# A graph-and-experts kernel: eight column sums of the count matrix move from GpSimd to VectorE, between its comparisons

## The chip, the cores and the metric

The kernel runs on one core of a Trainium2 chip. The metric is the device time of one execution in microseconds (us), the median of three runs. The profile is of one execution, taken by the hardware profiler. The engines are called TensorE (PE in the rows, PEld for its weight loads), VectorE (DVE), ScalarE (ACT), GpSimd (POOL) and SyncE (SP, which here only issues DMAs).

## The reference

The input x has 1250 nodes of 512 features; src and dst name 40,000 edges, sorted by dst. Two residual layers follow each other:

```python
def gnn(x):                                  # on layernorm(x)
    h = relu(x @ W1 + b1) @ W2 + b2          # 512 -> 256 -> 512
    agg = segment_sum(h[dst], src, 1250)     # edge_index = (src, dst)
    return h + agg
x = x + gnn(layernorm(x))

def moe(t):                                  # on layernorm(x), 8 experts of 512 x 512
    gate = softmax(t @ W_gate + b_gate)
    adapted = gate - 0.25 * sigmoid(t @ W_thr + b_thr)
    weights = max(adapted, 0) / sum          # 1 where the sum is 0
    return sum_e weights[e] * (t @ W_exp[e] + b_exp[e])
x = x + moe(layernorm(x))
```

With A[d, s] the number of edges from src s to dst d plus the identity, the aggregation is a product with A, and the bias b2 enters each node once for each edge and once for itself: it is multiplied by the column sums of A. These column sums are what the change is about.

## The kernel before

The 1250 nodes are 10 tiles of 125. Row tile i of A is built from five windows of 25 destination rows, so there are 50 windows, `w` from 0 to 49, and tile i consists of windows 5i to 5i+4.

For each window the engines do this:
- VectorE, `compare(w)` (line 556): equality comparisons (line 570) of the edge keys with the positions of the window. They write one-hot blocks in f16 into the ring `hot`. A window has 3 parts up to window 8, then 2 parts: 4 and 4 blocks up to window 17 (125x1536 elements each), 3 and 3 up to window 29 (125x1152), 3 and 2 from window 30 on (125x1152 and 125x768). From window 9 on, the ring has four places, so that `compare(w)` waits until TensorE has used the blocks of window w-4 (`freed_by`, line 569). It also waits for `pos_ready`, the positions that ScalarE prepares five windows ahead.
- TensorE, `count(w)` (line 780 on): an opening matmul (line 791), one matmul for each block (line 798), which waits for the comparison, and a closing one (line 803).
- ScalarE copies the counts from PSUM into `counts` (line 399) and then prepares positions for window w+5 (line 374).
- SyncE moves the 25 rows of the window by DMA into `a_t[i % 3]` (line 285), with one semaphore `win_moved[q]` for each of the five windows of a tile. Before the first window of a tile from tile 3 on, it waits until the buffer's last tile has been used, by `g_done` and by `a_summed` (line 284).

Between windows TensorE also does the first layer (transposes at line 755, `hidden` at line 764) and the aggregation, `aggregate` (line 776), that multiplies the relu'd features by the rows of `a_t`. Aggregation of tile i runs in five pieces behind windows 5i+8 to 5i+12, three windows behind the last window of the tile. Its fifth piece is the longest, with four matmuls.

GpSimd forms the sum of the rows of all tiles, `a_sum`, in the loop of lines 357 to 361: for tiles 1 to 8 it waits until the five windows of the tile are moved (`moved`), and adds `a_t[i % 3]` to `a_sum`, 125x1250 elements in f32. GpSimd has no other work at that time. The addition of tile 9 is on VectorE already (line 599), behind its last comparison, one low-weights step for the gate (line 589) and one for expert 0 (line 593). TensorE then reduces `a_sum` over partitions (line 819), VectorE copies the result to `deg1` (line 601) and adds b2 times it to x (line 607).

After that come the second product (line 832), the second layer norm with its transposes (line 842), the gate, and the eight experts with three matmuls for each product (lines 868 to 870).

VectorE's order of work is written out in the loop at line 581: `compare(w)`, then for some windows `statistics` or `normalise1`. Each engine executes its instructions in this order. `normalise1((w-1)//2)` follows `compare(w)` for odd w up to 19.

Of the kernel before, what the change touches and what calls it, by code (L numbers as in the profile page):

```python
# [16 lines left out]
ALU = mybir.AluOpType  # L17
# [13 lines left out]
def gnn_moe(nc, x, src, dst, W1, b1, W2, b2, Wg, bg, Wt, bt, We, be, out):  # L31
# [4 lines left out]
    TILES = 10  # L36
# [11 lines left out]
    WPT = 5  # L48
# [19 lines left out]
    with ExitStack() as ctx:  # L68
# [3 lines left out]
        def sem(name):  # L72
            return ctx.enter_context(nc.semaphore(name))
# [82 lines left out]
        a_t = [late[:, i * SW:(i + 1) * SW] for i in range(3)]  # L156
        a_sum = late[:, 3 * SW:4 * SW]
# [57 lines left out]
        a_summed = sem("a_summed")  # L215
# [20 lines left out]
        def parts_of(w):  # L236

            return next(parts for end, parts in STEPS if w < end)

        def hot_at(w, p):  # L240

            if w < EARLY:
                return 4 * (w % 2) + p
            return 2 * ((w - EARLY + 2) % 4) + p

        def freed_by(w):

            return w - 2 if w < EARLY + 2 else w - 3 if w < EARLY + 4 else w - 4

        def moved(eng, tile):  # L250

            for q in range(WPT):
                eng.wait_ge(win_moved[q], 16 * (tile + 1))
# [60 lines left out]
        @block.gpsimd  # L314
        def _(pool):
            nc.gpsimd.memset(ident[:, :], 0.0).then_inc(const_base, 1)
            nc.gpsimd.memset(ones[:, :], 1.0).then_inc(const_ready, 1)
            nc.gpsimd.memset(eps[:, :], LN_EPS).then_inc(const_ready, 1)
            nc.gpsimd.iota(base_row[:, :], pattern=[[WIN, NW]], base=0, channel_multiplier=0,
                           allow_small_or_imprecise_dtypes=True).then_inc(const_ready, 1)  # L320
            nc.gpsimd.iota(last_row[:, :], pattern=[[WIN, NW]], base=WIN - 1, channel_multiplier=0,
                           allow_small_or_imprecise_dtypes=True).then_inc(const_ready, 1)
            nc.gpsimd.iota(c_up[:, :], pattern=[[ROWS, GJ]], base=1, channel_multiplier=1,
                           allow_small_or_imprecise_dtypes=True).then_inc(const_ready, 1)
            nc.gpsimd.iota(c_down[:, :], pattern=[[-ROWS, GJ]], base=CH, channel_multiplier=-1,
                           allow_small_or_imprecise_dtypes=True).then_inc(const_ready, 1)
            pool.wait_ge(const_base, 1)
            nc.gpsimd.affine_select(out=ident[:, :], in_=ident[:, :], compare_op=ALU.not_equal, fill=1.0,
                                    base=0, pattern=[[-1, 128]], channel_multiplier=1).then_inc(const_ready, 1)

            nc.gpsimd.memset(step_col[:, :], float(sum(STEPS[-1][1]))).then_inc(step_base, 1)
            for n in range(len(STEPS) - 1, 0, -1):
                pool.wait_ge(step_base, len(STEPS) - n)
                nc.gpsimd.affine_select(out=step_col[:, :], in_=step_col[:, :], compare_op=ALU.is_ge,
                                        fill=float(sum(STEPS[n - 1][1])), base=-STEPS[n - 1][0], pattern=[[0, 1]],
                                        channel_multiplier=1).then_inc(step_base, 1)

            nc.gpsimd.iota(iota_lo[:, :], pattern=[[1, 2 * SEG]], base=0, channel_multiplier=0,
                           allow_small_or_imprecise_dtypes=True).then_inc(lo_ready, 1)
            nc.gpsimd.iota(iota_pos[:, :, 0:WIN * HI], pattern=[[0, PART], [1, WIN * HI]], base=0, channel_multiplier=0,  # L340
                           allow_small_or_imprecise_dtypes=True).then_inc(lo_ready, 1)
            nc.gpsimd.memset(iota_pos[:, :, WIN * HI:SEG], -20000).then_inc(lo_ready, 1)
            nc.gpsimd.iota(win_base[:, :], pattern=[[WIN * HI, NW]], base=0, channel_multiplier=0,
                           allow_small_or_imprecise_dtypes=True).then_inc(lo_ready, 1)
            nc.gpsimd.memset(keys[:, CH * REC:(CH + PADS) * REC], -1).then_inc(lo_ready, 1)

            nc.gpsimd.memset(zeros[:, :], 0.0).then_inc(self_ready, 1)
            nc.gpsimd.memset(self_pos[:, :], 0.0).then_inc(self_base, 1)
            nc.gpsimd.memset(self_lo[:, :], 0.0).then_inc(self_base, 1)
            pool.wait_ge(self_base, 2)  # L350

            nc.gpsimd.affine_select(out=self_pos[0:WIN, :], in_=self_pos[0:WIN, :], compare_op=ALU.not_equal, fill=1.0,
                                    base=-(HI - 1), pattern=[[1, SEG + HI - 1]], channel_multiplier=-HI).then_inc(self_ready, 1)
            nc.gpsimd.affine_select(out=self_lo[0:WIN, :], in_=self_lo[0:WIN, :], compare_op=ALU.not_equal, fill=1.0,
                                    base=-(LO - WIN), pattern=[[1, 2 * LO - WIN]], channel_multiplier=-1).then_inc(self_ready, 1)

            for i in range(1, TILES - 1):
                moved(pool, i)
                if i > 1:
                    pool.wait_ge(a_summed, i - 1)  # L360
                nc.gpsimd.tensor_tensor(a_sum, a_t[0] if i == 1 else a_sum, a_t[i % 3], ALU.add).then_inc(a_summed, 1)  # L361

        @block.scalar
        def _(act):
            act.dma_start(x_sb[112:R, :, :], x.rearrange("(t p) d -> p t d", p=R)[112:R, :, :]).then_inc(x_rest, 16)
# [101 lines left out]
        def _(dve):  # L467
# [56 lines left out]
            def statistics(half):  # L524
                for i in range(half * TILES // 2, (half + 1) * TILES // 2):
                    dve.wait_ge(x_in[i // 2], 16)
                    if i == 0:
                        dve.wait_ge(x_rest, 16)
                    nc.vector.bn_stats(stats1[:, i, :], x_sb[:, i, :]).then_inc(ln1_stats, 1)  # L529
                for i in range(half * TILES // 2, (half + 1) * TILES // 2):  # L530
                    dve.wait_ge(ln1_stats, i + 1)
                    nc.vector.bn_aggr(mv1[:, i, :], stats1[:, i, :]).then_inc(ln1_mv, 1)
# [23 lines left out]
            def compare(w):  # L556

                word = dve.snap(word_reg)
                parts = parts_of(w)
                dve.reg_add(need_reg, end_reg[freed_by(w) % 4], 1)  # L560
                dve.wait_ge(pos_ready, w + 1)
                if w < WPT:
                    dve.wait_ge(lo_ready, 6 + w)
                with dve.Fori(word % WORD, word // WORD, sum(parts) * REC) as k:
                    for p, n in enumerate(parts):
                        key_at = nc.s_assert_within(
                            k + sum(parts[:p]) * REC, 0, (CH + PADS - n) * REC,
                            skip_runtime_bounds_check_because="the table gives a block only steps that begin below CH")
                        dve.wait_ge(hot_used[p], dve.snap(need_reg))
                        nc.vector.tensor_tensor(hot[hot_at(w, p)][:, 0:n, :].rearrange("p c (k x j) -> p (c k) x j", k=SEGS, j=2),  # L570
                                                places[w % WPT][:, 0:n, :].rearrange("p c (k x j) -> p (c k) x j", k=SEGS, j=2),
                                                keys[:, ds(key_at, n * REC)].rearrange("p (k j) -> p k j", j=2).unsqueeze(2)
                                                .broadcast_to([EP, n * SEGS, SEG // 2, 2]),
                                                ALU.is_equal).then_inc(hot_ready[p], 1)

                    dve.reg_load(word_reg, wtab[0:1, w + 1:w + 2])
                    dve.reg_add(turn_reg, turn_reg, 1)
                    dve.reg_add(need_reg, turn_reg, 1)
                dve.reg_mov(end_reg[w % 4], turn_reg)

            for w in range(NW):
                compare(w)
                if w < 2:
                    statistics(w)
                if 1 <= w < 1 + 2 * TILES and (w - 1) % 2 == 0:
                    normalise1((w - 1) // 2)
# [7 lines left out]
                                               op0=ALU.mult, op1=ALU.subtract).then_inc(we_lo_done, 1)  # L594

            low_weights(0, 0)
            moved(dve, TILES - 1)
            dve.wait_ge(a_summed, TILES - 2)
            nc.vector.tensor_tensor(a_sum, a_sum, a_t[(TILES - 1) % 3], ALU.add).then_inc(a_summed, 1)
            dve.wait_ge(deg_done, 1)  # L600
            nc.vector.tensor_copy(deg1[:, :], ps_a[0:R, 0:TILES]).then_inc(deg_ready, 1)
            dve.wait_ge(deg_ready, 1)
# [326 lines left out]
```

## Time and profile before

| what | value |
|---|---|
| median of 3 runs | 419.51 us (419.5 to 421.23) |
| the profiled execution's own time | 421.23 us |
| its span in the profile | 419.4 us |
| TensorE busy | 390.8 us, 93% |
| VectorE busy | 294.9 us, 70% |
| ScalarE busy | 102.2 us, 24% |
| GpSimd busy | 26.3 us, 6% |

The span is the time from the first to the last instruction that the profile shows. Busy time is that of the instructions of an engine; register, branch, semaphore and DMA-issuing instructions are not in it. In the slices of the page, each digit is the busy share of a fortieth of the span (10.5 us) in tenths.

### The profile page before, as it was taken

To read this page: it belongs to the slowest core of one execution; us is meant where nothing else is said; L and a number is where in the kernel's file an instruction comes from. 1 tells how busy PE (TensorE), PEld (TensorE's weight loads), DVE (VectorE), ACT (ScalarE), POOL (GpSimd) and SP (SyncE) were. 2 spreads that over 40 slices of the span, in tenths; PEclk is the share of its full clock that TensorE was granted. 3 is DMA by queue.
4 is the path that set the end of the run, shared out by engine and by line. 5 is a ranking of instruction groups with operands and counts; after the bars stand their busy time and mean duration, and the time that the engine had idled before them with its cause. 6 is when DMAs were issued, how large, how long until landed. Compare 5 with 4: busy or idle time off the path is not lost.

```text
span 419.4 us, 6001 instructions
## 1 busy us (share of the span) xinstructions
PE 390.8 (93%) x1943; PEld 244.8 (58%) x1943; DVE 294.9 (70%) x438; ACT 102.2 (24%) x176; POOL 26.3 (6%) x35
## 2 busy tenths in 40 slices
PE   0845999999999999899799999999999999999996
PEld 0422676666656555546566666666666666666663
DVE  3799999945677993698359666575765757657653
ACT  4621243434456551245430101001010010100000
POOL 4000000210222223000000000000000000000000
PEclk9998699999999999999699999999999999999999
DMA  8500013214124222162001102030020300000133
GB/s 182 143 12 13 18 37 103 56 37 133 40 65 155 76 72 74 22 171 106 0 2 45 56 1 100 2 100 0 0 100 0 100 0 0 0 0 0 50 98 98
DMA packets 16681, 23.75 MB, mean 57 GB/s; under 512 B 2792, under 2 KB 9555, under 8 KB 16532
## 3 DMA queue, kind: packets, MB, share of 16 engines
q1 hardware_dynamic: 16254, 22.93, 18.7%
q10 hardware_dynamic: 403, 0.53, 0.6%
q8 instruction: 12, 0.20, 0.2%
q14 instruction: 12, 0.10, 0.1%
HBM read 14.65 MB, written 2.56 MB: 41 GB/s over the span
## 4 chain that ended last, share of the span: by engine, by line
PE 86%; DVE 8%; DMA 2%; issue 1%; DVEq 1%; ACT 1%; ACTq 0%
PE ps_g L868 17%; PE ps_g L870 17%; PE ps_g L869 17%; PE ps_w L798 10%; PE ps_g L776 10%; PE ps_a L764 5%; PE ps_g L832 2%; DVE split L570 2%; DVE x_sb L607 1%; PE ps_a L765 1%; PE ps_a L755 1%; DVE stats L529 1%; DMA dst_i<-in_dst_dram 1%; PE ps_w L791 1%; PE ps_w L803 1%
## 5 line engine op out<-in xcount | busy, mean ns | idle before, releaser
L868 PE MATMUL ps_g<-we_hi,split 128*125 128x512 f16 x320 | 122.4, 383 | 0.0
L869 PE MATMUL ps_g<-we_lo,split 128*125 128x512 f16 x320 | 122.0, 381 | 0.0
L870 PE MATMUL ps_g<-we_hi,split 128*125 128x512 f16 x320 | 122.0, 381 | 0.0
L570 DVE TENSOR_TENSOR split<-places,keys 125x1536 f16<-125x1536 int16 (+2 forms) x125 | 106.8, 916 | 17.6 <-PE ps_w L798 11.5
L681 DVE SCALAR_TENSOR_TENSOR x_sb<-ps_g,weight_s,x_sb 125x512 f32<-125x512 f32 x80 | 60.0, 750 | 56.2 <-PE ps_g L870 56.1
L798 PE MATMUL ps_w<-split 125*128 125x250 f16 x416 | 60.3, 288 | 10.8 <-DVE split L570 10.8
L686 DVE SCALAR_TENSOR_TENSOR x_sb<-late,weight,x_sb 125x512 f32<-125x512 f32 x80 | 60.0, 751 | 9.5 <-DVE x_sb L681 4.9
L798 PEld LDWEIGHTS ps_w<-split 125*128 125x128 f16 x416 | 40.5, 102 | 32.4 <-DVE split L570 19.0
L868 PEld LDWEIGHTS ps_g<-we_hi,split 128*125 128x125 f16 x320 | 44.1, 138 | 25.9 <-issue 0.6
L870 PEld LDWEIGHTS ps_g<-we_hi,split 128*125 128x125 f16 x320 | 44.0, 137 | 25.9 <-issue 0.8
L869 PEld LDWEIGHTS ps_g<-we_lo,split 128*125 128x125 f16 x320 | 44.1, 138 | 25.4 <-issue 0.6
L776 PE MATMUL ps_g<-late,r_sb 125*128 125x512 f32 (+3 forms) x120 | 53.0, 545 | 0.6 <-DMA late<-counts 0.6
L443 ACT ACTIVATE we_hi<-stage 128x2048 f16<-128x2048 f32 x6 | 11.5, 1912 | 139.4 <-PE ps_g L870 139.4
L399 ACT ACTIVATE counts<-ps_w 128x250 f32<-128x250 f32 x50 | 19.0, 379 | 70.6 <-PE ps_w L803 70.6
L374 ACT ACTIVATE places<-iota_pos,win_base 125x512 int16<-125x512 int16 x50 | 35.6, 713 | 0.0
L361 POOL TENSOR_TENSOR late<-late 125x1250 f32<-125x1250 f32 x8 | 21.2, 2649 | 135.4 <-DMA late<-counts 135.4
L776 PEld LDWEIGHTS ps_g<-late,r_sb 125*128 125x128 f32 x120 | 19.2, 189 | 10.0 <-issue 9.4
L764 PE MATMUL ps_a<-w_sb,xn_t 128*125 128x256 f32 x80 | 19.9, 392 | 0.0
L593 DVE SCALAR_TENSOR_TENSOR we_lo<-stage,we_hi 128x2048 f16<-128x2048 f32 x8 | 18.3, 2284 | 0.0
L764 PEld LDWEIGHTS ps_a<-w_sb,xn_t 128*125 128x125 f32 x80 | 14.2, 187 | 1.8
L832 PE MATMUL ps_g<-w_sb,early 128*125 128x512 f32 x32 | 14.8, 595 | 0.1
L791 PE MATMUL ps_w<-self_lo,self_pos 128*128 128x250 f16 x50 | 13.9, 278 | 0.0
(127 smaller groups left out, 200.2 us busy)
## 6 DMA issues: line engine op xcount, KB each, us to landing
stage<-in_L_ffn_W_exp_dram SPq DMA_DIRECT2D x8, 1024.0 KB, 5.3
late<-counts SPq DMA_DIRECT2D x50, 122.1 KB
x_sb<-in_x_dram SPq DMA_DIRECT2D x5, 448.0 KB, 9.4
out_dram<-x_sb SPq DMA_DIRECT2D x10, 224.0 KB
late<-in_L_ffn_b_exp_dram SPq DMA_DIRECT2D x1, 2000.0 KB
w_sb<-in_L_gnn_W_dram SPq DMA_DIRECT2D x2, 512.0 KB, 8.3
x_sb<-in_x_dram ACTq DMA_DIRECT2D x1, 260.0 KB
out_dram<-x_sb ACTq DMA_DIRECT2D x10, 26.0 KB
```

Source lines behind the costliest of these rows:

```text
L361: nc.gpsimd.tensor_tensor(a_sum, a_t[0] if i == 1 else a_sum, a_t[i % 3], ALU.add).then_inc(a_summed, 1)
L374: nc.scalar.activation(places[w % WPT][:, :, 0:SEG], iota_pos[:, :, :], ACT.Identity, bias=win_base[:, w:w + 1], scale=1.0).then_inc(pos_r ...
L570: nc.vector.tensor_tensor(hot[hot_at(w, p)][:, 0:n, :].rearrange("p c (k x j) -> p (c k) x j", k=SEGS, j=2), places[w % WPT][:, 0:n, :].re ...
L681: nc.vector.scalar_tensor_tensor(out=x_sb[:, i, :], in0=ps_exp[(TILES * par + i) % RING], scalar=weight_s[:, ds(e, 1), i], in1=x_sb[:, i, ...
L686: nc.vector.scalar_tensor_tensor(out=x_sb[:, i, :], in0=be_sb[:, ds(e, 1), :], scalar=weight[:, i, ds(e, 1)], in1=x_sb[:, i, :], op0=ALU.m ...
L764: nc.tensor.matmul(ps_a[0:R, 0:C], xn_t[:, k, :], w1_sb[:, k, :], start=(k == 0), stop=False)
L776: g = nc.tensor.matmul(ps_g[:, a:z], r_sb[:, i, c * 128:(c + 1) * 128], a_t[i % 3][:, a - c * SW:z - c * SW], start=False, stop=False, ski ...
L798: mm = nc.tensor.matmul(bank[:, 0:LO], hot[hot_at(w, p)][:, c, 0:SEG], hot[hot_at(w, p)][:, c, SEG:SEG + LO], start=False, stop=False, ski ...
L832: y = nc.tensor.matmul(ps_y[i % YS], g_sb[:, c, tokens[i]], w2_sb[:, c, :], start=(c == 0), stop=(c == KC - 1))
L868: nc.tensor.matmul(bank, xhi[:, k, tokens[i]], hi_w, start=(k == 0), stop=False)
L869: nc.tensor.matmul(bank, xhi[:, k, tokens[i]], lo_w, start=False, stop=False)
L870: mm = nc.tensor.matmul(bank, xlo[:, k, tokens[i]], hi_w, start=False, stop=(k == KD - 1))
```

## The change

GpSimd's loop goes away. VectorE gets a function `column_sum(i)` with the same waits and the same addition. It is called for tiles 1 to 8 in the loop over windows: after `compare(w)` for w = 12, 17, ..., 47, with i = 1, 2, ..., 8; that is, three windows after the last window of tile i. Tile 9's sum, already on VectorE, is now written as a call of the same function in the same place.

```diff
@@ GpSimd @@
-            for i in range(1, TILES - 1):
-                moved(pool, i)
-                if i > 1:
-                    pool.wait_ge(a_summed, i - 1)
-                nc.gpsimd.tensor_tensor(a_sum, a_t[0] if i == 1 else a_sum, a_t[i % 3], ALU.add).then_inc(a_summed, 1)
@@ VectorE @@
+            def column_sum(i):
+
+                moved(dve, i)
+                if i > 1:
+                    dve.wait_ge(a_summed, i - 1)
+                nc.vector.tensor_tensor(a_sum, a_t[0] if i == 1 else a_sum, a_t[i % 3], ALU.add).then_inc(a_summed, 1)
+
             for w in range(NW):
                 compare(w)
+                if w >= 2 * WPT + 2 and (w - 2) % WPT == 0:
+                    column_sum((w - 2) // WPT - 1)
                 if w < 2:
                     statistics(w)
@@ VectorE, after the loop @@
             low_weights(0, 0)
-            moved(dve, TILES - 1)
-            dve.wait_ge(a_summed, TILES - 2)
-            nc.vector.tensor_tensor(a_sum, a_sum, a_t[(TILES - 1) % 3], ALU.add).then_inc(a_summed, 1)
+            column_sum(TILES - 1)
```

## Rows read from the trace of the kernel before

**Rows 1.** The page's slices of the span: VectorE busy, and TensorE's granted clock.

```profile
DVE  3799999945677993698359666575765757657653
...
PEclk9998699999999999999699999999999999999999
```

**Rows 2.** The page's chain that ended last, shares by engine.

```profile
PE 86%; DVE 8%; DMA 2%; issue 1%; DVEq 1%; ACT 1%; ACTq 0%
```

**Rows 3.** Busy time by stretch: start:end, length, PE busy, clock, DMA share.

```profile
70.00:164.00 94.00, 94.00 (x500) 1.00 0.28 84
...
202.90:208.60 5.70, 5.66 (x22) 0.50 0.00 0
```

**Rows 4.** What TensorE waited for, in 0 to 60 us.

```profile
PE ps_w L798 <- DVE split L570: 10.8, 12, 4.0
```

**Rows 5.** The same, in 60 to 180 us.

```profile
PE ps_g L776 <- DMA late<-counts: 0.6, 1, 0.6
```

**Rows 6.** Chain in order of time, after the last window.

```profile
165.00 3.39 DMA late<-counts
```

**Rows 7.** Timeline of GpSimd: start, length, instruction, idle before it.

```profile
75.65 2.40 POOL L361 TENSOR_TENSOR late<-late 125x1250 f32<-125x1250 f32 x1 [69.27 <-DMA late<-counts]
...
123.24 3.01 POOL L361 TENSOR_TENSOR late<-late 125x1250 f32<-125x1250 f32 x1 [12.56 <-DMA late<-counts]
133.70 2.40 POOL L361 TENSOR_TENSOR late<-late 125x1250 f32<-125x1250 f32 x1 [7.45 <-DMA late<-counts]
142.23 2.42 POOL L361 TENSOR_TENSOR late<-late 125x1250 f32<-125x1250 f32 x1 [6.14 <-DMA late<-counts]
150.56 2.83 POOL L361 TENSOR_TENSOR late<-late 125x1250 f32<-125x1250 f32 x1 [5.91 <-DMA late<-counts]
159.65 3.34 POOL L361 TENSOR_TENSOR late<-late 125x1250 f32<-125x1250 f32 x1 [6.25 <-DMA late<-counts]
```

**Rows 8.** Timeline of VectorE at tile 1.

```profile
69.92 3.56 DVE L570 TENSOR_TENSOR split<-places,keys 125x1536 f16<-125x1536 int16 x4
...
74.84 5.77 DVE L570 TENSOR_TENSOR split<-places,keys 125x1536 f16<-125x1536 int16 x4
```

**Rows 9.** Timeline of VectorE, two pairs of comparisons, low weights, tile 9's sum.

```profile
114.43 1.43 DVE L570 TENSOR_TENSOR split<-places,keys 125x1152 f16<-125x1152 int16 x2 [1.13 <-PE ps_w L798]
...
148.26 1.23 DVE L570 TENSOR_TENSOR split<-places,keys 125x1152 f16<-125x1152 int16 x2 [0.25 <-PE ps_w L798]
...
158.45 2.28 DVE L593 SCALAR_TENSOR_TENSOR we_lo<-stage,we_hi 128x2048 f16<-128x2048 f32 x1
168.61 1.46 DVE L599 TENSOR_TENSOR late<-late 125x1250 f32<-125x1250 f32 x1 [7.88 <-DMA late<-counts]
```

**Rows 10.** Timeline of ScalarE: evictions of windows 24, 29, 34, 49.

```profile
119.39 0.38 ACT L399 ACTIVATE counts<-ps_w 128x250 f32<-128x250 f32 x1 [0.93 <-PE ps_w L803]
...
128.86 0.38 ACT L399 ACTIVATE counts<-ps_w 128x250 f32<-128x250 f32 x1 [0.93 <-PE ps_w L803]
...
137.80 0.38 ACT L399 ACTIVATE counts<-ps_w 128x250 f32<-128x250 f32 x1 [0.82 <-PE ps_w L803]
...
164.60 0.38 ACT L399 ACTIVATE counts<-ps_w 128x250 f32<-128x250 f32 x1 [1.42 <-PE ps_w L803]
```

**Rows 11.** Timeline of TensorE: closing matmuls of windows 28, 33, 38, 43, 48.

```profile
126.68 0.17 PE L803 MATMUL ps_w<-zeros 1*128 1x2 f16 x1
...
135.72 0.17 PE L803 MATMUL ps_w<-zeros 1*128 1x2 f16 x1
...
144.66 0.17 PE L803 MATMUL ps_w<-zeros 1*128 1x2 f16 x1
...
153.59 0.17 PE L803 MATMUL ps_w<-zeros 1*128 1x2 f16 x1
...
162.52 0.17 PE L803 MATMUL ps_w<-zeros 1*128 1x2 f16 x1
```

**Rows 12.** The same: the eight counting matmuls of window 13.

```profile
82.22 1.02 PE L798 MATMUL ps_w<-split 125*128 125x250 f16 x8
```

## The prediction

> **What bounds the kernel now.** I read four views in this order. The chain that ended last is TensorE for 86% of the span and VectorE for 8% [rows 2]. The stage that the change touches, from the first addition on GpSimd at 75.65 us to window 49 at 164 us, has TensorE busy without a gap, 94.00 of 94.00 us, at full clock [rows 3]. The list of waits agrees: TensorE waited for comparisons 10.8 us in all, but all of it before 60 us [rows 4]; after 60 us the longest entry is 0.6 us for a DMA [rows 5]. VectorE is far from idle there, its slices run from 3 to 9 tenths [rows 1], but it is ahead of TensorE. Behind window 49 a different thing sets the pace: its rows are copied at 164.60, moved by DMA for 3.39 us from 165.00 on [rows 6, 10], and only then can the last pieces of the aggregation and tile 9's column sum (168.61) start [rows 9].
>
> So time can be won in this stage only where TensorE waits, and it does not. Time is lost wherever VectorE, now with more to wait for, hands over blocks late.
>
> **What is removed.** Eight additions on GpSimd, 2.40 us each where nothing disturbs them [rows 7]. None is on the chain: the last starts at 159.65 and ends at 162.99, 5.6 us before tile 9's sum needs it at 168.61. Their removal is worth 0 us directly.
>
> They do cost VectorE time. Four comparisons of 125x1536 take 3.56 us when GpSimd is idle, and 5.77 us when the addition of 75.65 lies among them, 2.21 us more [rows 7, 8]. The Trainium skill has a rule for this (SBUF — State Buffer, "Who interferes with whom"): a VectorE instruction with two SBUF inputs and a GpSimd instruction that reads SBUF exclude each other, and the second waits out the first. The trace agrees, by 2.21 of 2.40 us. Whether the rule moves the end is a matter of what VectorE's time is worth, and here it is worth nothing by [rows 3 to 5].
>
> **What is added.** Eight additions on VectorE. Tile 9's sum is the same operation on the same engine: 1.46 us [rows 9]. VectorE pays 8 x 1.46 = 11.7 us and gets back up to 8 x 2.21 = 17.7 us. In sum its load falls by about 6 us. That is not the point, though: the additions also bring a wait, and all that stands behind it in VectorE's order waits too: `compare` of the next windows, and for tile 2 `normalise1(8)`.
>
> How long is the wait? `column_sum(i)` follows `compare(5i+7)` and waits for the DMA of window 5i+4. GpSimd's addition waits for the same DMA and starts as soon as it has landed, so its start is the landing: 75.65, 123.24, 133.70, 142.23, 150.56, 159.65 for tiles 1, 4, 5, 6, 7, 8 [rows 7]. The ring lets VectorE run four windows ahead, so it will be at the wait before that. The question for each tile is whether `compare(5i+8)`, which can begin only at landing + 1.46, is still in time for TensorE.
>
> Tile 1: `compare(13)` is ready at 75.65 + 1.46 + two comparisons at 3.56/4 = 0.89 each, 78.9. TensorE's matmuls of window 13 begin at 82.22 [rows 12]. Over 3 us to spare; 0 us lost. Tiles 2 and 3, read in the same way, have more, since transposes and the first layer lie between the windows. `normalise1(8)` feeds a transpose behind window 18; it moves to after tile 2's sum and stays in time.
>
> Tiles 4 to 8 are tighter. The transposes and the first layer are over, and TensorE takes only 8.9 us for five windows [rows 11]. I compute when TensorE could close window 5i+8: landing + sum 1.46 + both comparisons + the matmuls of the second part + the handover.
> - From window 30 on the pair of comparisons takes 1.23 us [rows 9]; the second part has two matmuls, at 1.02/8 = 0.13 us each [rows 12], 0.25 us, and the handovers I take as nothing, since comparisons follow each other with an overlap of about the same size. The constant is 2.94 us.
> - Window 28 (tile 4) has the pair of 1.43 us [rows 9] and three matmuls, 0.38 us: 3.27 us.
>
> Against the closing matmuls of before [rows 11]:
> - Tile 4: 123.24 + 3.27 = 126.51, before 126.68: hidden, with 0.17 to spare.
> - Tile 5: 133.70 + 2.94 = 136.64, before 135.72: 0.92 late.
> - Tile 6: 142.23 + 2.94 = 145.17, before 144.66: 0.51 late.
> - Tile 7: 150.56 + 2.94 = 153.50, before 153.59: hidden, 0.09 to spare.
> - Tile 8: 159.65 + 2.94 = 162.59, before 162.52: 0.07 late.
>
> A delay of TensorE shifts everything behind it, landings too, so the later rows hold relative to each other, and the delays add up: 0.92 + 0.51 + 0.07 = 1.50 us. Between the sums VectorE catches up: it needs 1.23 us for a window from 30 on, where TensorE needs 8.94/5 = 1.79 us [rows 9, 11]; five comparisons and a sum are 7.6 us of these 8.9. So no lag carries over.
>
> Why are tiles 5 and 6 late? From the start of the eviction to the landing it is 3.85 us for window 24, but 4.84 us for window 29 and 4.43 us for window 34 [rows 7, 10]; window 49 took 4.01 [rows 9, 10]. This gives the bounds of the unknown cost. With every landing as quick as window 24's, tiles 5 and 6 end at 128.86 + 3.85 + 2.94 = 135.65 and 144.59, both in time: 0 us. With every landing as slow as window 29's, tile 4 is 0.82 late and each of the four others, on the same schedule, 0.92: 4.50 us. I take what the rows of these very tiles show, 1.50 us.
>
> **At the end of the stage.** `compare(48)` and `compare(49)` now follow tile 8's sum: 159.65 + 1.46 + 2 x 1.23 = 163.6. The low-weights step of 2.28 us behind them [rows 9] ends near 166, with the small one for the gate, and tile 9's sum waits for its DMA until 168.61 anyway [rows 9]. Cost 0 us; without that cover, it would be the 1.5 us or so that they would stick out. SyncE's wait on `a_summed` before it overwrites a buffer asks for a sum that is two tiles old; the sums end earlier than on GpSimd (1.46 against 2.40 us), so it is never late.
>
> **Sum.** 421.23 + 1.50 = 422.7 us for the profiled execution's own time (span 419.4 + 1.5 = 420.9). That execution is 1.7 us above the median of its runs; the same 1.5 us on the median of 419.51 give 421.0 us.
>
> **The rivals.**
> - *All hidden.* The landings come quickly, or VectorE is a few tenths quicker than I reckon; nothing sticks out. For it: margins and delays of tiles 4, 7 and 8 are all under 0.2 us, and one of the two real delays rests on a single slow landing. Against it: window 34's landing was slow as well. 419.5 us.
> - *VectorE late at every tile from 4 on.* The wait takes VectorE's lead away once in five windows, and each time TensorE stands at the next window. It decides as soon as a landing comes more than 3.9 us behind the start of its eviction (tile 5: 135.72 - 2.94 = 132.78, less 128.86). For it: three of the five landings worked out above are beyond that. Against it: tiles 4 and 7. Its price is the upper bound, 4.5 us: 424.0 us. This is the slower side.
> - *VectorE's time is worth something after all.* Every addition on GpSimd held up comparisons for up to 2.21 us [rows 8]. If TensorE, whose ends are modelled, was held too in each case, the change gives back 8 x (2.21 - 1.46) = 6.0 us: 413.5 us. For it: the stretched comparison at 74.84. Against it: 94 us without a gap [rows 3, 5]. [...]
> - *The clock.* At 202.9 us TensorE's granted clock is at its lower level, 1.2 GHz, for 5.7 us, after a stretch with pauses [rows 1, 3]. If the shifted work missed that fall, it would win some half of 5.7, 2.9 us: 421.0 - 2.9 = 418.1 us. For it: 1.7 us separate the runs of before already. Against it: nothing in the change bears on that stretch but its time of arrival.
>
> **How the numbers follow.** Forecast, tiles 5 and 6 late: 0.44. All hidden: 0.20. Late everywhere: 0.25. VectorE relief: 0.06. Clock: 0.05. About 0.5% is what a measurement of this kernel can tell from no change, 2.1 us: 417.4 to 421.6. Faster: the relief case and a little of the clock, 0.08. Slower: late everywhere, and 0.05 of the forecast's own spread beyond 421.6, 0.30. Same: the rest, 0.62. Range: from 418.0, which takes in the clock case and leaves out the relief, to 424.0, the upper bound; with part of the late case beyond it, less than 2 in 10 is left out.
>
> **What would show it.** GpSimd has no L361 rows. There are eight VectorE additions of about 1.46 us (if 2 us or more, the term for the sum is wrong), each begun within 0.3 us of its window's landing, with idle time of VectorE before it that a DMA ended. No comparison is stretched to 3 us. In the waits of TensorE after 60 us there is a new entry for comparisons, of about 1 us in the middle of windows 33 and 38, none at windows 13, 18, 23. Window 49 closes about 1.5 us later, and the expert passes are as long as before. The prediction is wrong if TensorE waits at all tiles from 4 on, or if the closing of window 49 stays where it was, or comes earlier.

## The result, and the profile after

| | median (us) | runs |
|---|---|---|
| before | 420.36 | 5, 419.5 to 421.41 |
| changed | 423.86 | 5, 422.15 to 424.24 |

The ratio is 1.0065, with an interval of 1.0038 to 1.0094. A second set, with 12 runs of the changed kernel, gave 422.76 against 420.51, ratio 1.0055 (1.0032 to 1.0078). The change makes the kernel slower, by 2.3 to 3.5 us in the medians.

The page of the changed kernel, its span, slices and chain, to be read beside [rows 1, 2]:

```profile
span 420.5 us, 6007 instructions
...
DVE  4799997855646886698459666575665757657653
...
PEclk9986899999999999999699999999999999999999
...
PE 82%; DVE 9%; DMA 3%; issue 3%; DVEq 2%; ACT 1%; ACTq 0%
```

TensorE's share of the chain is down from 86 to 82%, and what came in its place is spread over DMA, VectorE and issue. The list of waits of TensorE in 60 to 180 us (waiting engine, line and releaser; us in total, times, longest) has one new entry beside that of [rows 5]:

```profile
PE ps_w L799 <- DVE split L564: 1.3, 1, 1.3
PE ps_g L777 <- DMA late<-counts: 0.5, 1, 0.5
```

The list of VectorE for the same time shows the new waits, nine with tile 9's:

```profile
DVE late L580 <- DMA late<-counts: 28.9, 9, 5.2
```

VectorE waits 28.9 us in all for landings, and TensorE pays for it in one visible place, 1.3 us. The timeline of VectorE (start, length, instruction, idle before it) has the sums of tiles 1, 4 to 8 and 9, with the comparisons after the first:

```profile
74.84 1.46 DVE L580 TENSOR_TENSOR late<-late 125x1250 f32<-125x1250 f32 x1 [3.90 <-DMA late<-counts]
76.22 1.82 DVE L564 TENSOR_TENSOR split<-places,keys 125x1536 f16<-125x1536 int16 x2
...
122.39 1.46 DVE L580 TENSOR_TENSOR late<-late 125x1250 f32<-125x1250 f32 x1 [4.67 <-DMA late<-counts]
...
133.53 1.46 DVE L580 TENSOR_TENSOR late<-late 125x1250 f32<-125x1250 f32 x1 [2.64 <-DMA late<-counts]
...
142.51 1.46 DVE L580 TENSOR_TENSOR late<-late 125x1250 f32<-125x1250 f32 x1 [1.43 <-DMA late<-counts]
...
151.62 1.46 DVE L580 TENSOR_TENSOR late<-late 125x1250 f32<-125x1250 f32 x1 [1.14 <-DMA late<-counts]
...
160.57 1.46 DVE L580 TENSOR_TENSOR late<-late 125x1250 f32<-125x1250 f32 x1 [1.80 <-DMA late<-counts]
...
169.68 1.46 DVE L580 TENSOR_TENSOR late<-late 125x1250 f32<-125x1250 f32 x1 [3.07 <-DMA late<-counts]
```

Each sum is 1.46 us, as [rows 9] had it, and what follows starts 0.08 us before the end. No comparison is stretched any more: 1.82 us for two of 125x1536, where [rows 8] had 5.77 for four.

The closing matmuls of TensorE for windows 10, 28, 32, 33, 38, 43, 48 and 49, to be read beside [rows 11]:

```profile
72.77 0.17 PE L804 MATMUL ps_w<-zeros 1*128 1x2 f16 x1
...
125.87 0.17 PE L804 MATMUL ps_w<-zeros 1*128 1x2 f16 x1
...
132.37 0.17 PE L804 MATMUL ps_w<-zeros 1*128 1x2 f16 x1
...
136.51 0.17 PE L804 MATMUL ps_w<-zeros 1*128 1x2 f16 x1
...
145.55 0.17 PE L804 MATMUL ps_w<-zeros 1*128 1x2 f16 x1
...
154.69 0.17 PE L804 MATMUL ps_w<-zeros 1*128 1x2 f16 x1
...
163.63 0.17 PE L804 MATMUL ps_w<-zeros 1*128 1x2 f16 x1
...
165.45 0.17 PE L804 MATMUL ps_w<-zeros 1*128 1x2 f16 x1
```

Set against the kernel before, window by window, this locates the loss. Windows 3 to 32 all close 0.79 to 0.81 us earlier than before: that much this execution had won before window 3, where the two kernels do the same, so it is not counted as an effect of the change. Window 33 closes 0.79 us later than before. So 1.58 us are lost at this one window; 0.10 more at window 34, 0.21 at window 39, and at 43 and 48 nothing. From window 10 to window 49 the kernel before took 164.33 - 73.57 = 90.76 us and the changed one 165.45 - 72.77 = 92.68: the stage costs 1.92 us. Behind window 49 both need 255.1 us to the end of the span, so the spans differ by 1.92 - 0.81 = 1.1 us. The experiments are read by this gap from window 10 to window 49, as it leaves out what varies from execution to execution before and after. TensorE's granted clock is 1.00 all through the gap in both profiles, and in those of all the experiments but load_w36 and earlier1.

The chain in order of time (start, length, what) goes through tile 5's sum:

```profile
128.07 0.39 ACT counts L393
...
128.48 4.84 DMA late<-counts
...
133.53 0.08 DVE late L580
...
134.26 0.66 DVEq L570
134.91 0.76 DVE split L564
...
135.72 0.86 PE ps_w L799 x5
```

It reads from top to bottom: eviction of window 29, 4.84 us of DMA, the sum, 0.66 us of VectorE's sequencer while the sum runs, the first comparison of window 33, and then TensorE's matmuls. The evictions of windows 29, 34 and 49, beside [rows 10]:

```profile
128.07 0.38 ACT L393 ACTIVATE counts<-ps_w 128x250 f32<-128x250 f32 x1 [0.94 <-PE ps_w L804]
...
138.69 0.38 ACT L393 ACTIVATE counts<-ps_w 128x250 f32<-128x250 f32 x1 [0.92 <-PE ps_w L804]
...
165.72 0.38 ACT L393 ACTIVATE counts<-ps_w 128x250 f32<-128x250 f32 x1 [1.44 <-PE ps_w L804]
```

From the start of the eviction to the sum it is 133.53 - 128.07 = 5.46 us for window 29, and 142.51 - 138.69 = 3.82 us for window 34.

### The profile page after: what moved, and what is told of

It is laid out like the page before. It is cut to its first block, busy times and chain, and to the rows that moved or that the text cites. A ratio compares the mean times of both kernels' runs of the same rounds, so it can differ in the third digit from the quotient of the medians.

```text
span 420.5 us, 6007 instructions
## 1 busy us (share of the span) xinstructions
PE 391.4 (93%) x1943; PEld 244.1 (58%) x1943; DVE 293.0 (70%) x446; ACT 102.1 (24%) x176; POOL 5.1 (1%) x27
## 4 chain that ended last, share of the span: by engine, by line
PE 82%; DVE 9%; DMA 3%; issue 3%; DVEq 2%; ACT 1%; ACTq 0%
PE ps_g L869 17%; PE ps_g L871 17%; PE ps_g L870 17%; PE ps_g L777 9%; PE ps_w L799 8%; PE ps_a L765 5%; DVE split L564 3%; PE ps_g L833 2%; DMA late<-counts 2%; DVE x_sb L608 1%; PE ps_a L766 1%; DVE stats L523 1%; DMA dst_i<-in_dst_dram 1%; PE ps_a L756 1%; PE ps_w L792 1%
## 5 line engine op out<-in xcount | busy, mean ns | idle before, releaser
L564 DVE TENSOR_TENSOR split<-places,keys 125x1536 f16<-125x1536 int16 (+2 forms) x125 | 94.4, 820 | 7.6 <-PE ps_w L799 4.2
L580 DVE TENSOR_TENSOR late<-late 125x1250 f32<-125x1250 f32 x9 | 13.2, 1461 | 28.9 <-DMA late<-counts 28.9
```

## The experiments

Two theories were on the table after this. By L and Q together, VectorE's wait for a landing with the sum behind it passes its lead over TensorE at tile 5, where the landing is late because it shares the DMA queue with the load of expert 1's weights. By W, VectorE has no room for the work. All gaps are those from the close of window 10 to the close of window 49; the kernel before has 90.76 us, the changed one 92.68.

| kernel | gap (us) | jump at window 33 | ratio to before |
|---|---|---|---|
| changed | 92.68 | 1.58 | 1.0065 (1.0038 to 1.0094) |
| changed, again | 92.79 | 1.65 | 1.0055 (1.0032 to 1.0078) |
| later1 | 90.75 | 0 | 0.9999 (0.9978 to 1.0021) |
| later5 | 90.75 | 0 | 0.9997 (0.9975 to 1.0019) |
| no_sums | 90.76 | 0 | 0.9994 (0.997 to 1.0018) |
| wait_nosum | 92.97 | 2.11 | 1 run |
| wait_nosum_w20 | 90.76 | 0 | 1 run |
| load_w20 | 91.67 | 0 | 1.0002 (0.9984 to 1.0019) |
| load_w36 | 95.64 | 0 | 1 run |
| load_end | 91.39 | 0 | 1.0044 (1.0026 to 1.0062) |
| earlier1 | 109.48 | at 27 to 47 | 1 run |
| before_w36 | 90.75 | 0 | 1 run |

**later1**, one window more of lead.

```diff
-                if w >= 2 * WPT + 2 and (w - 2) % WPT == 0:
-                    column_sum((w - 2) // WPT - 1)
+                if w >= 2 * WPT + 3 and (w - 3) % WPT == 0:
+                    column_sum((w - 3) // WPT - 1)
```

> The changed kernel with each of the eight sums one window later: column_sum(i) after compare(5i+8). Theory L (the wait for the landing of window 5i+4 and the 1.46 us sum behind it together pass VectorE's lead at tile 5): one window more of lead, 1.33 to 1.8 us, covers the 1.58 us of tile 5, so the gap between the closes of windows 10 and 49 is that of the kernel before (90.76 us), to within 0.3 us, and the time is 1.9 us under the changed kernel's. Theory W (VectorE has no room for eight sums of 1.46 us, wherever they are): the gap stays at 92.7 us, and the time at the changed kernel's. Theory C (what the runs show is only the clock at 30 to 50 and 202 to 212 us): the gap is short or long without order.

The closing matmuls of windows 10 and 49:

```profile
73.35 0.17 PE L804 MATMUL ps_w<-zeros 1*128 1x2 f16 x1
...
164.10 0.17 PE L804 MATMUL ps_w<-zeros 1*128 1x2 f16 x1
```

The gap is that of the kernel before, to 0.01 us, and so is the time (421.05 against 420.93 us). Theory L holds its number; theory W is out.

**later5**, the work of the sums without any wait but tile 8's and 9's.

```diff
-                if w >= 2 * WPT + 2 and (w - 2) % WPT == 0:
-                    column_sum((w - 2) // WPT - 1)
+                if w >= 3 * WPT + 2 and (w - 2) % WPT == 0:
+                    column_sum((w - 2) // WPT - 2)
@@ after the loop @@
+            column_sum(TILES - 2)
             low_weights(0, 0)
             column_sum(TILES - 1)
```

> The changed kernel with each sum five windows later: column_sum(i) after compare(5i+12), tile 8's after the last comparison. All of a tile's windows have landed by then, so the sums bring work and no wait. Theory L: 0 us; gap of windows 10 to 49 of 90.8 us. Theory W: 92.7 us, the work alone costs it. One more addition stands ahead of the low weights; they end at some 163 us, well before the last landing, cost 0.

```profile
72.82 0.17 PE L805 MATMUL ps_w<-zeros 1*128 1x2 f16 x1
...
163.57 0.17 PE L805 MATMUL ps_w<-zeros 1*128 1x2 f16 x1
```

The closing matmuls of windows 10 and 49 are 90.75 us apart again. The sums are free on VectorE when they don't wait: seven of the eight stand between comparisons here, and tile 8's behind the last.

**wait_nosum**, the waits without the work.

```diff
-                    column_sum((w - 2) // WPT - 1)
+                    moved(dve, (w - 2) // WPT - 1)
```

Beyond these lines, SyncE's wait on `a_summed` is gone, and the addition behind the loop adds two other tiles, `a_t[0]` and `a_t[1]`. The same holds for no_sums and wait_nosum_w20, so all three leave tiles out of the degree.

> The changed kernel with the waits of column_sum(1) to (8) on VectorE and in their places, but without the eight additions (the sum over tiles 1 to 8 is left out of the degree; tile 9's addition stays, on other data). Theory L: tile 5's 1.58 us shrink by the 1.46 us of the sum to 0.1 to 0.2 us, tile 6's 0.2 go: gap 90.8 to 91.0 us. A theory that the wait alone costs it (sequencer restart after a DMA wait): 92 us or more. Theory W: 90.8.

This missed. The gap is 92.97 us, which by the text above is the number of the theory that the wait alone costs it. The eviction of window 29 on ScalarE, the first comparison after the wait on VectorE, and the close of window 33 on TensorE:

```profile
128.66 0.38 ACT L392 ACTIVATE counts<-ps_w 128x250 f32<-128x250 f32 x1 [0.93 <-PE ps_w L804]
```

```profile
136.01 1.23 DVE L563 TENSOR_TENSOR split<-places,keys 125x1152 f16<-125x1152 int16 x2 [4.32 <-DMA late<-counts]
```

```profile
137.62 0.17 PE L804 MATMUL ps_w<-zeros 1*128 1x2 f16 x1
```

The first comparison begins 136.01 - 128.66 = 7.35 us after the eviction. That is not the landing itself, since a comparison begins a little later behind a wait than a sum does. Tile 4 shows by how much: its eviction and its first comparison in this trace are

```profile
119.19 0.38 ACT L392 ACTIVATE counts<-ps_w 128x250 f32<-128x250 f32 x1 [0.92 <-PE ps_w L804]
```

```profile
123.38 1.43 DVE L563 TENSOR_TENSOR split<-places,keys 125x1152 f16<-125x1152 int16 x2 [5.05 <-DMA late<-counts]
```

4.19 us apart, where the changed kernel's sum of tile 4 began 122.39 - 118.58 = 3.81 us after its eviction: 0.38 us. So on the scale of the sums tile 5's landing took 7.35 - 0.38 = 6.97 us here, an estimate, 1.5 us more than the 5.46 of the changed kernel. Leaving out the sum saves less than its 1.46 us: in the changed kernel the comparison begins 134.91 - 133.53 = 1.38 us after the sum does, so 1.38 - 0.38 = 1.0 us is saved. The two together, 1.5 - 1.0 = 0.5 us, are what the jump grew by, from 1.58 to 2.11 us. So this run doesn't speak against L, but it shows that tile 5's landing varies, and it left open what a wait costs at a usual landing. wait_nosum_w20, below, answers that.

**no_sums**, neither work nor wait, on no engine.

> The changed kernel without the eight sums and without their waits, on no engine (they are left out of the degree). The floor of this stage: if GpSimd's additions cost the kernel before nothing, the gap of windows 10 to 49 is its 90.76 us and the time is within 0.3% of it. If VectorE's held-up comparisons (2.2 us for each addition on GpSimd) cost the end anything, it is up to 6 us faster.

The closes of windows 10 and 49 are at 72.83 and 163.59: a gap of 90.76 us, and 0.9994 of the time of before. So GpSimd's additions cost the stage of the kernel before nothing, in spite of the comparisons that they held up. With nothing to win from their removal, no placing of these eight sums should make the stage shorter than it was.

**load_w36 and load_end**, the load of expert 1's weights elsewhere.

```diff
-                if w == 26:
+                if w == 36:                  # load_end: if w == 49:
                     load_expert(1)
```

> The changed kernel with the load of expert 1's weights (1 MB on SyncE's queue) behind window 36's move instead of window 26's. Theory Q (tile 5 is late because window 29's move stands in the DMA queue behind that load): window 33 closes without a jump against the kernel before (0 instead of 1.58 us), and the jump, 1 to 2 us, moves to window 43, since window 39 is now the one behind the load. Theory P (tile 5 is late for another reason, ScalarE's 1.9 us of high weights at window 30 or the change of part sizes at window 30): the jump stays at window 33.

The sums of tiles 5 and 7 on VectorE, and the eviction of window 39 on ScalarE:

```profile
132.58 1.46 DVE L580 TENSOR_TENSOR late<-late 125x1250 f32<-125x1250 f32 x1 [1.37 <-DMA late<-counts]
...
153.73 1.46 DVE L580 TENSOR_TENSOR late<-late 125x1250 f32<-125x1250 f32 x1 [3.59 <-DMA late<-counts]
```

```profile
147.35 0.38 ACT L393 ACTIVATE counts<-ps_w 128x250 f32<-128x250 f32 x1 [1.19 <-PE ps_w L804]
```

Tile 5's sum begins at 132.58, 0.95 us earlier than in the changed kernel, and window 33 has no jump. Tile 7's takes the load's effect: 153.73 - 147.35 = 6.38 us from eviction to landing. The jump came at window 43 as the theory says, 2.49 us, somewhat more than expected; windows 38 and 39 lost another 0.68. It went on over windows 44 and 45 to 4.18 us, and that part is the clock and not VectorE. Length, TensorE busy, granted clock, DMA share and GB/s from 157.8 to 161.2 us:

```profile
157.80:161.20 3.40, 3.40 (x10) 0.50 0.13 37
```

TensorE had been busy for only 1.82 of the 3.80 us before, and was then granted 0.50, its lower level of 1.2 GHz, for these 3.4 us. Half of 3.4 is 1.7, an estimate, and windows 44 and 45 lose 0.82 and 0.87. TensorE's list of waits in this stage has one wait for comparisons, 2.2 us. Theory P, that the place is bound to window 30 or 33, is out.

> The changed kernel with the same load behind window 49's move. Theory Q: no jump over 0.3 us at any window, the gap of windows 10 to 49 is 90.8 to 91.2 us, and the time is some 1.7 us under the changed kernel's, level with the kernel before. Theory P: gap of 92.7 us. If the later arrival of expert 1 mattered, the expert passes would begin late; the first of them takes some 20 us, so nothing of that is expected.

The sums of tiles 5 and 9 on VectorE, and TensorE's waits from 160 us on:

```profile
132.42 1.46 DVE L580 TENSOR_TENSOR late<-late 125x1250 f32<-125x1250 f32 x1 [1.40 <-DMA late<-counts]
...
170.75 1.46 DVE L580 TENSOR_TENSOR late<-late 125x1250 f32<-125x1250 f32 x1 [5.02 <-DMA late<-counts]
```

```profile
PE ps_g L777 <- DMA late<-counts: 2.5, 2, 2.3
```

The stage is nearly free of loss. It is 0.63 us over before, 0.2 more than expected, with 0.20 us each at windows 34, 39 and 49. But the expectation for the time failed: the ratio is 1.0044. Window 49's move was issued ahead of the load and still came later, its sum at 170.75, 6.02 us after the close of window 49 at 164.73, against 4.28 us before. That landing is on the path, and TensorE waited 2.3 us for it. Then its granted clock was 0.50 from 171.2 to 174.4 us, and the four matmuls behind the wait took 3.46 us, against 1.95 in the changed kernel. Behind window 49 this execution needs 258.1 us, and the kernel before 255.1. A load behind a move in the queue slowed the move too.

**earlier1**, one window less of lead (`(w - 1)` in place of `(w - 2)`).

> The changed kernel with each sum one window earlier, column_sum(i) after compare(5i+6). The lead when the landing is awaited is one window less, so the late hand-over grows by the distance of two windows: 1.3 to 1.8 us where four matmuls of the aggregation don't lie between. Tiles 4 to 8 then lose 2.6 (window 27 closes 124.01, 2.67 us before window 28), and tiles 5 to 8 2.56 us more each than now: gap of windows 10 to 49 of about 92.7 + 5 x 2.5 = 105 us at most; if only the excess over the margin counts, some 102 us. A theory that the sums' place is of no matter: 92.7 us.

TensorE's waits for comparisons in 60 to 185 us, and the close of window 49:

```profile
PE ps_w L799 <- DVE split L564: 10.7, 5, 2.2
```

```profile
182.24 0.17 PE L804 MATMUL ps_w<-zeros 1*128 1x2 f16 x1
```

The gap grew by 16.8 us over the changed kernel's, the run took 439.2 us. The direction is as expected, and the size beyond the most I had allowed (105 us): against the kernel before, tiles 4 to 7 lost 3.7 to 4.2 us each, over two windows (27 and 28, 32 and 33, and so on), and tile 8 2.5 at window 47. Not all of it is VectorE's lateness. TensorE's granted clock was 0.50 from 124.8 to 128.0, 138.4 to 141.7, 152.1 to 155.3 and 165.7 to 169.0 us, each time behind one of its waits; the fifth wait was followed by no fall. Half of these 13.0 us is 6.5 us, an estimate; with the 10.7 us of waits that is 17.2 of the 18.7 us over before. Two windows of lead span all there is: 18.7 us at one place, 1.9 at the next, 0 from the third on.

The load stood behind window 26's move here too, and yet tile 5's landing was a usual one, 135.76 - 131.95 = 3.81 us. Windows 27 and 28 had been late, so that window 29 closed 9.8 us after window 26, where it is 6.1 in the changed kernel, and the load had more time. This fits theory Q.

**after_again**, the changed kernel again.

> The changed kernel itself again, for the scatter of window 29's landing and of the stage: by theory Q its jump at window 33 varies from execution to execution between 0.9 and 2.3 us with the time at which the load has drained, and the ratio to the kernel before stays between 1.003 and 1.008.

The jump at window 33 was 1.65 us, the gap 92.79 us; the ratio lies in the expected span. Together with wait_nosum there are jumps of 1.58, 1.65 and 2.11 us.

This profiled execution took 424.55 us, the first one 422.29, with the gap only 0.1 us longer. The rest stands behind window 49, from where it is 257.2 us to the end of the span instead of 255.1. The stretch from 175.0 to 181.6 us (length, TensorE busy, granted clock, DMA share, GB/s) in the first profile of the changed kernel and in this one:

```profile
175.00:181.60 6.60, 6.02 (x15) 1.00 0.55 137
175.00:181.60 6.60, 6.13 (x8) 0.50 0.38 86
```

The granted clock was at its lower level for the whole stretch, and the four matmuls of the second product at 177.81 took 3.78 us, where those at 176.79 had taken 1.98. The kernel before had 1.00 there. But later5, whose gap has no loss, had 0.50 from 171.9 to 175.1 us, so such a fall is not shown to come from the change.

**load_w20**, the load where the windows are far apart.

> The changed kernel with the load of expert 1's weights behind window 20's move, where TensorE takes about 10 us from window 20 to window 24 and nothing is queued close behind it. Theory Q: the load has drained before window 24's move, no landing of a tile's last window is late, gap of windows 10 to 49 is 90.8 to 91.4 us (load_end, whose stage was free of the load, had 91.39), and the last landing is undisturbed, so that the time is level with the kernel before (ratio 0.998 to 1.003). If only the distance to the tile's last window counts (four windows here, as few as three for window 26 to 29), tile 4 is late by 0.5 to 1 us instead.

Tile 5's sum on VectorE, and the chain about window 34:

```profile
131.91 1.46 DVE L580 TENSOR_TENSOR late<-late 125x1250 f32<-125x1250 f32 x1 [1.92 <-DMA late<-counts]
```

```profile
136.33 0.33 issue
136.65 0.70 PE ps_w L799 x5
```

From the eviction at 128.09 it is 3.82 us, and window 33 has no jump. The DMA share and GB/s (last two columns, after length and clock) of 123 to 129 us in the changed kernel, and the same in load_w20:

```profile
123.00:129.00 6.00, 1.00 0.68 213
```

```profile
123.00:129.00 6.00, 1.00 0.25 73
```

With the load at window 26 the 16 DMA engines are busy for 68% of the time up to 129 us, and for 34% from there to 133, which I read as the held-up moves going through; without it both are at a quarter. The time is level with before (421.18 against 421.0 us), so moving one load takes the loss of time back within what the runs can tell. In the stage it does so only in part. The gap was 91.67 us, 0.91 over before and 0.27 above what I had expected: windows 34, 39 and 49 lose 0.53, 0.16 and 0.20 us. Of the first, 0.33 stands in TensorE's own issue by the chain, though the comparisons of window 34 were done by 135.7; the list of waits puts the same 0.33 down to the comparisons. What TensorE's sequencer does there isn't settled.

**before_w36**, GpSimd's sums and the load at window 36.

> The kernel before, sums on GpSimd, with the load behind window 36's move. Theory L (a landing costs only where VectorE waits for it in front of comparisons): GpSimd waits instead, the gap of windows 10 to 49 stays at 90.76 us, though window 39's move lands as late as in load_w36 (whose jump was 2.5 us at window 43, 4.2 us by window 45). If the late moves held up ScalarE's evictions or SyncE, the kernel before would lose something too: 92 us or more.

Tile 7's addition on GpSimd, and the close of window 49 (window 10 closed at 73.20):

```profile
153.19 2.83 POOL L361 TENSOR_TENSOR late<-late 125x1250 f32<-125x1250 f32 x1 [8.78 <-DMA late<-counts]
```

```profile
163.95 0.17 PE L803 MATMUL ps_w<-zeros 1*128 1x2 f16 x1
```

The landing was later than in load_w36 (153.19, with the eviction at 146.35: 6.84 us), and the gap stays at 90.75 us. A late landing costs nothing as long as the engine that waits for it has nothing else to do.

**wait_nosum_w20**, the waits alone, the load at window 20.

> The waits of column_sum(1) to (8) on VectorE without the eight additions (they are left out of the degree), with the load behind window 20's move. Theory L with Q: a wait alone, for landings of usual length, passes no lead: gap 90.76 us. If a wait costs by itself, in the engine's restart, some tenths of a us at tiles 5 to 8: 91.2 us or more.

The gap is 90.76 us. Waits for landings of usual length cost nothing in this execution. The same waits with the sums behind them (load_w20) cost 0.91 us of the stage, so wait and sum together are not quite free even at usual landings.

## Why the prediction was right, and where its sizes were off

- *TensorE bounds the stage, and removing GpSimd's additions is worth 0.* Right: no_sums has the gap of before to the hundredth.
- *VectorE's load falls by about 6 us.* The size is wrong. 2.21 us for each addition was taken from one of them. The comparisons together went from 106.8 to 94.4 us busy, 12.4 us for all eight, and the sums took 11.7 us, so VectorE's busy time fell by only 1.9 us, from 294.9 to 293.0. Nothing in the forecast hung on it.
- *The sum on VectorE is 1.46 us, and the work is covered.* Right: 1.46 us in every case, and later5 costs 0.
- *Only tiles 4 to 8 are tight; the close comes 2.94 us after the landing.* The constant held: landing 133.53 gives 136.47, and window 33 closed at 136.51. The constant came from the parts' durations with nothing for handovers; the chain shows 0.66 us of sequencer time that hides behind the sum, and wait_nosum shows that a comparison begins 0.38 us later behind a wait than a sum would.
- *Tile 5 late by 0.92 us.* The mechanism and the place are right and the size is off, 1.58 us. The term that was mis-sized is the landing. I took 4.84 us from the eviction to the landing from the single execution of before; it was 5.46 in the changed kernel, 5.52 when that was run again, and about 7.0 in wait_nosum. I noted that this landing was slow, and did not ask why. The load of 1 MB issued three windows ahead was in the trace, and it makes this landing a draw from a spread and not a constant. Of the stage's 1.92 us, moving the load away takes back 1.0 to 1.3 (load_w20 and load_end keep 0.91 and 0.63).
- *Tile 6 late by 0.51 us.* Wrong: 0 at window 38, 0.21 at window 39. That 0.21 is no late comparison; 0.16 of it is issue of TensorE ahead of the aggregation's piece, as at 39 in load_end, where no landing was late. Tile 6's landing took 3.82 us, where before it had 4.43. So the landings after a delay don't all shift rigidly with it, as I had reckoned. The load doesn't explain the 4.43: before_w36, which issues it later, has 142.02 - 137.42 = 4.60 us. That the delay at window 33 gave the queue time to empty is a likely reason, not a shown one.
- *Tile 8 late by 0.07, tiles 4 and 7 hidden, nothing lost behind window 49.* Right within 0.1 us in the first profile; the second lost 2.2 us behind window 49, at the lower clock.
- *Sum 1.50 us.* The stage lost 1.92 and 2.03 us in the two profiles. The medians moved by 3.5 and 2.3 us. The difference of 0.2 to 1.6 us is not in the stage. Part of it may be the lower clock from 175.0 to 181.6 us, which only the second profile shows, in an execution 2.3 us longer than the first; one profile of each kernel can't tell whether the changed kernel takes such a fall more often. Runs of the kernel before differ by up to 5 us among themselves, and the profiled executions by 0.9 us ahead of window 3.
- *421.0 us for the median, in a range from 418.0 to 424.0.* The medians were 423.86 and 422.76 us. The first lies 0.14 us inside the range, and there is luck in that: 0.85 us of the distance to the forecast is that the kernel before had a median of 420.36 and not 419.51, and the upper edge was the price of a rival, VectorE late at every tile, that did not come about. The 422.29 us of the profiled execution, close to the 422.7 forecast for it, are luck too, since 0.8 us had been won ahead of window 3.
- *Chances.* I gave 0.62 to a move within 0.5%, on 1.50 us against a bound of 2.1; both measured moves, 3.5 and 2.3 us, are beyond it. With a cost that could only grow from there, by a landing of unknown spread, slower deserved more than its 0.30.

The rival of all hidden failed at tile 5, that of VectorE late everywhere at tiles 4, 6, 7 and 8. VectorE's relief is shown to be worth 0. The clock was granted in the same way from 196 to 214 us before and after, 0.81 on average, so the gain of that rival didn't come about; the second profile shows the clock working the other way, from 175.0 us on.

## What to carry to other kernels

When work moves from an idle engine to a busy one, look at its waits before its duration: here the work alone cost 0, the wait alone cost 0 while the landing was on time, and the two together cost 0.6 to 0.9 us of the stage at usual landings, for a reason that stays open; behind a late landing the wait, with or without the work, passed the lead. Look at the clock before a loss is put down to a wait: in load_w36 a wait of 2.2 us was followed by 1.7 us more at the lower clock. An engine with nothing else to do absorbed a late DMA for nothing (before_w36). Place such a step where the data has surely landed; one window later made it free. And take a landing time that the sum rests on from more than one row, and look what else is in the queue at that time.

## What the runs showed of the hardware

- A 1 MB load in the queue stretched the landing of a 122 KB move issued three windows behind it from 3.8 us (start of the eviction to start of the sum) to 4.8 and 5.5 us, and to about 7.0 by an estimate for wait_nosum, in different executions.
- It also stretched a move issued ahead of it: 6.02 us instead of 4.28 from close to sum, with the load issued right behind (load_end, one profile).
- TensorE's granted clock fell from 1.00 to 0.50 behind waits of about 2 us in load_w36, load_end and earlier1, for 3.2 to 3.4 us each time. Behind the wait of 1.3 us in the changed kernel it stayed at 1.00, and so it did behind the last wait of earlier1. What decides it isn't shown.
- A GpSimd addition of 125x1250 f32 held up four of VectorE's comparisons by 2.21 us at tile 1; at tile 7 a single comparison of 125x768 took 3.21 us, where the shortest took 0.55, so 2.66 us more. The Trainium skill's rule on the shared port (SBUF — State Buffer, "Who interferes with whom") agrees. That this time was worth nothing at the end is shown by no_sums.
